# Cross-attention and expert layers on one core: the maxima's mask, the layer norms' root, the counts of a threshold search and a value bias are computed in another way

## The reference, cut to what matters

```python
x = x + attention0(layernorm(x), ctx)             # no mask
x = x + expert_choice(layernorm(x))               # 8 experts, each takes its 1024 best tokens
x = x + attention1(layernorm(x), ctx, mask, pad)  # mask (512 x 64), pad (16 x 64)
x = x + zone_mixture(layernorm(x))                # 8 experts, all tokens

layernorm(x) = (x - mean) / sqrt(var + 1e-5)
# attention1:
V = ctx @ wv.T + bv
attn = softmax(where(pad, where(mask, Q @ K.T / 4, -1e8), -1e8))
out = (attn @ V) @ wo.T + bo
# expert_choice:
Sm = softmax(x @ Wr + br); G, idx = top_k(Sm.T, 1024)
```

## Time and profile before

| | |
|---|---|
| median of three runs | 2231.78 us |
| the profiled execution | 2222.29 us |
| its span in the trace | 2220.6 us |
| TensorE busy | 2063.2 us, 93% |
| VectorE busy | 1386.9 us, 62% |
| ScalarE busy | 937.7 us, 42% |
| GpSimd busy | 357.7 us, 16% |
| attention of layer 0 | 0 to about 378 us |
| search and lists | about 378 to 453 us |
| expert choice's mixture | about 453 to 737 us |
| attention of layer 1 | about 737 to 1140 us |
| zone mixture | from there to the end |

### The profile page before, as it was taken

One profiled execution on the slowest core, in us unless ns is written; L12 is line 12 of the kernel. 1 busy time (PEld: TensorE's weight loads), 2 busy tenths in 40 slices (PEclk: granted clock), 3 DMA queues, 4 the chain that ended last, 5 costly groups with the idle time before them and its releaser, 6 DMA issues.

```text
span 2220.6 us, 38835 instructions
## 1 busy us (share of the span) xinstructions
PE 2063.2 (93%) x14664; PEld 1684.4 (76%) x14665; DVE 1386.9 (62%) x2859; ACT 937.7 (42%) x1405; POOL 357.7 (16%) x351
## 2 busy tenths in 40 slices
PE   7899997589999689999989999999999999999998
PEld 4666665369998456666668888888888888888887
DVE  6888886855555478888768554544545445445444
ACT  3777773055445266666643222222222222222222
POOL 3122211057774311111122000000000000000000
PEclk9999997789999799999989999999999999999999
DMA  3122222045543212222230000000000010010000
GB/s 102 59 85 77 84 68 56 4 128 110 94 78 51 57 39 71 71 72 71 96 133 24 25 29 29 29 29 11 19 29 29 29 29 1 29 29 29 29 10 10
DMA packets 109106, 114.11 MB, mean 51 GB/s; under 512 B 16064, under 2 KB 97728, under 8 KB 108992
## 3 DMA queue, kind: packets, MB, share of 16 engines
q1 hardware_dynamic: 96704, 95.44, 13.5%
q0 software_dynamic: 12288, 17.05, 4.8%
HBM read 61.87 MB, written 50.59 MB: 51 GB/s over the span
## 4 chain that ended last, share of the span: by engine, by line
PE 46%; DVE 2%; ACT 1%; issue 1%; DVEq 0%
PE psum L144 15%; PE psum L145 15%; PE psum L146 15%; DVE zmix_acc L2237 0%; DVE zmix_hid L2246 0%; ACT zmix_hid_hi L2202 0%; ACT L2194 0%; DVE zmix_rest_inh L1882 0%; ACT zmix_act_gate L2194 0%; DVE zmix_rest_zone L1887 0%; DVE zmix_rest_inh L1888 0%; DVE zmix_rest_key L1905 0%; DVE zmix_rest_flag L1907 0%; DVE zmix_rest_key L1904 0%; DVE zmix_rest_best L1906 0%
## 5 line engine op out<-in xcount | busy, mean ns | idle before, releaser
L2246 DVE TENSOR_TENSOR zmix_hid<-zmix_act_gate,psum 128x1024 f32<-128x1024 f32 x128 | 156.3, 1221 | 378.9 <-issue 350.9
L2202 ACT ACTIVATE zmix_hid_hi<-zmix_hid 128x1024 fp32r<-128x1024 f32 x128 | 135.6, 1059 | 394.1 <-PE psum L146 238.8
L2194 ACT ACTIVATE zmix_act_gate<-psum 128x1024 f32<-128x1024 f32 x128 | 131.4, 1027 | 376.3 <-PE psum L146 376.2
L2251 DVE TENSOR_TENSOR zmix_hid_lo<-zmix_hid,zmix_hid_hi 128x1024 fp32r<-128x1024 f32 x128 | 157.7, 1232 | 134.9 <-ACT zmix_hid_hi L2202 133.9
L144 PE MATMUL psum<-zmix_wd_hi,zmix_hid_hi 128*128 128x256 f32 x768 | 217.3, 283 | 2.2 <-DVE zmix_acc L2237 1.9
L145 PE MATMUL psum<-zmix_wd_lo,zmix_hid_hi 128*128 128x256 f32 x768 | 217.2, 283 | 0.0
L146 PE MATMUL psum<-zmix_wd_hi,zmix_hid_lo 128*128 128x256 f32 x768 | 217.1, 283 | 0.0
L2237 DVE SCALAR_TENSOR_TENSOR zmix_acc<-psum,opened_weight,zmix_acc 128x256 f32<-128x256 f32 x512 | 211.6, 475 | 1.6 <-PE psum L146 1.6
L929 ACT ACTIVATE att_probs<-psum 128x512 f32<-128x512 f32 x256 | 135.3, 601 | 92.2 <-PE psum L746 51.6
L1090 DVE TENSOR_REDUCE att_s_max<-psum 128x16 f32<-128x1024 f32 x128 | 152.8, 1216 | 20.6 <-PE psum L712 20.5
L144 PEld LDWEIGHTS psum<-zmix_wd_hi,zmix_hid_hi 128*128 128x128 f32 x768 | 146.8, 191 | 7.4 <-DVE zmix_hid_lo L2251 1.9
(11 more groups left out here) (396 smaller groups left out, 5529.5 us busy)
## 6 DMA issues: line engine op xcount, KB each, us to landing
x<-att_x_new SPq DMA_DIRECT2D x32, 512.0 KB, 2.9
att_x_in<-in_x SPq DMA_DIRECT2D x16, 512.0 KB, 4.0
rows<-att_normed_new SPq DMA_DIRECT2D x16, 512.0 KB, 3.0
att_x_in<-x SPq DMA_DIRECT2D x16, 512.0 KB, 3.9
turned<-att_newT SPq DMA_DIRECT2D x16, 512.0 KB, 2.8
zmix_acc<-x SPq DMA_DIRECT2D x16, 512.0 KB, 4.4
out_x<-zmix_acc SPq DMA_DIRECT2D x16, 512.0 KB, 3.2
moe_wd<-in_w_down SPq DMA_DIRECT2D x8, 768.0 KB, 5.9
```

The lines of the kernel that those rows point to most:

```text
L2194: act.activation(act_gate[:, :, :], psum[:, 0:2, :], ACT.Silu).then_inc(gate_out, 1)
L2202: act.activation(hid_hi[:, e % 2, :, :], hid[:, :, :], ACT.Copy).then_inc(hi_made, 1)
L2246: dve.tensor_tensor(hid[:, :, :], act_gate[:, :, :], psum[:, 2:4, :], ALU.mult).then_inc(up_out, 1)
L2251: dve.tensor_tensor(hid_lo[:, e % 2, :, :], hid[:, :, :], hid_hi[:, e % 2, :, :].bitcast(F32), ALU.subtract).then_inc(lo_made, 1)
```

## The change

Four edits, in both layers' attention, in the search, and in the set-up of layer 1. **Mask:** `masks` uses `mask_cur` as the 64-row stationary matrix and `keysel` as the moving one: 16 products of 64 rows and 128 columns, alternating between the two halves of the array's rows; `mask_tok`, its VectorE instruction, its two inputs and their conversions are gone. **Root:** `layernorm_means` ends with the aggregation; GpSimd (`roots`) adds eps, raises to the power -0.5, and makes the shift, four instructions, between `input_side` and the sum `x_bias`, which becomes `input_bias`; VectorE waits before an aggregation until the last `roots` has read the means. The openings of both layers keep the Newton steps. **Counts:** `count` and `same_e` are fp16. **Value bias:** in layer 1 ScalarE copies the value tiles out of PSUM, without bias; the bias, spread over lanes, is multiplied by `wo` in one product of each half and added to the output bias once.

```diff
+def layernorm_means(dve, xs, parts, stats, mv, sem, start, passed, before, mv_free):
...
+    dve.wait_ge(sem, start + n)
+    mv_free()
+    dve.sem_inc(passed, 1)
+    for k in parts:
+        for t in range(TT):
+            dve.bn_aggr(mv[:, k * TT + t, :], stats[:, k * TT + t, :]).then_inc(sem, 1)
...
-    shared["same_e"] = sc.sb("same_e", [P, E, CHUNKS], side="right")
+    shared["same_e"] = sc.sb("same_e", [P, E, CHUNKS], F16, side="right")
...
-            sp.dma_start(rows32[:, :, :], w["mask_rows"].rearrange("(t p) k -> p t k", p=P)).then_inc(mask_loaded, 16)
-            sp.dma_start(pads32[:, :, :].rearrange("p b k -> p (b k)"), w["pad_rows"].partition_broadcast(P)).then_inc(mask_loaded, 16)
...
-        dve.tensor_scalar(kv["pad_rows"][:, :, :], pads32[:, :, :].bitcast(U8), BIG, -BIG, ALU.mult, ALU.add)
-        dve.tensor_scalar(kv["mask_rows"][:, :, :], rows32[:, :, :].bitcast(U8), BIG, -BIG, ALU.mult, ALU.add)
...
+    def bias_rows(act):
+        for c in range(KC):
+            act.activation(bias_lanes[:, c, :], kv["bv"][:, c:c + 1].to_broadcast([P, P]), ACT.Copy).then_inc(bias_spread, 1)
+
+    def values_copy(act, b):
+        if b == 0:
+            act.wait_ge(v_cleared, 2)
+        act.wait_ge(v_made, b + 1)
+        for a in range(2):
+            rows = slice(a * SK, (a + 1) * SK)
+            heads = psum[rows, v_bank + b % V_BANKS, 0:D].rearrange("p (j a c) -> p j a c", a=2, c=DH)[:, :, a, :]
+            act.activation(kv["v"][rows, b, :, 0:DH], heads, ACT.Copy).then_inc(v_out, 1)
+
+    def value_bias(pe):
+        pe.wait_ge(bias_spread, KC)
+        for c in range(KC):
+            m = pe.matmul(psum[:, 0, 0:D], bias_lanes[:, c, :], wo[:, c, :], start=(c == 0), stop=(c == KC - 1))
+        m.then_inc(bias_made, 1)
+
+    def output_bias(dve):
+        dve.wait_ge(bias_made, 1)
+        dve.tensor_tensor(kv["bo"][:, :], psum[:, 0, 0:D], kv["bo"][:, :], ALU.add).then_inc(bias_out, 1)
...
+            def roots(b):
+                ahead, new = there(b + 2), there(b - 1)
+                pool.wait_ge(ln, ln_start(b) + mean_steps(ahead + new))
...
+                r, s = rstd[:, cols], shift[:, cols]
+                pool.tensor_scalar(r, mv[:, cols, 1], LN_EPS, None, ALU.add).then_inc(rooted, 1)
+                pool.wait_ge(rooted, b * 3 + 1)
+                pool.tensor_tensor(r, r, minus_half[:, cols], ALU.pow).then_inc(rooted, 1)
+                pool.tensor_scalar(s, mv[:, cols, 0], -1.0, None, ALU.mult).then_inc(rooted, 1)
+                pool.wait_ge(rooted, b * 3 + 3)
+                pool.tensor_tensor(s, s, r, ALU.mult).then_inc(shifted, 1)
...
             def body(b, p, half):
                 if there(b + 1):
                     input_side(b + 1, 1 - p, half + p)
+                if there(b + 2) or there(b - 1):
+                    roots(b)
+                if there(b + 1):
+                    input_bias(b + 1, 1 - p, half + p)
...
             def masks(p):
-                for j in range(PAIR_ROWS):
-                    pe.matmul(psum[:, 2 + j, :], const["ident16"][:, :],
-                              mask_tok[:, p, :, :].unsqueeze(2).to_broadcast([P, TT, 2, SK]), start=True, stop=False)
+                for t in range(TT):
+                    for j in range(PAIR_ROWS):
+                        keys = slice(j % 2 * SK, (j % 2 + 1) * SK)
+                        pe.matmul(psum[:, 2 + j, t * P:(t + 1) * P], mask_cur[keys, p, t * P:(t + 1) * P], const["keysel"][keys, :, :],
+                                  start=t == 0, stop=False)
...
-                pads = kv["pad_rows"][:, bass.ds(b, 1), :].to_broadcast([P, TT, SK])
-                dve.tensor_tensor(mask_tok[:, p, :, :], kv["mask_rows"][:, :, :], pads, ALU.min).then_inc(mask_ready, 1)
...
-                layernorm_stats(dve, xs, parts, stats, mv, rstd, tmp, ln, ln_start(b), passed, before)
-                dve.wait_ge(ln, ln_start(b) + steps)
-                cols = slice(0 if ahead else TT, 2 * TT if new else TT)
-                dve.scalar_tensor_tensor(shift[:, cols], mv[:, cols, 0], -1.0, rstd[:, cols], ALU.mult, ALU.mult).then_inc(shifted, 1)
+                layernorm_means(dve, xs, parts, stats, mv, ln, ln_start(b), passed, before, lambda: dve.wait_ge(shifted, b + 1))
...
-        count = sc.sb("count", [P, 1])
+        count = sc.sb("count", [P, 1], F16)
...
             setup["high_parts"](act)
+            setup["bias_rows"](act)
+            for b in range(B):
+                setup["values_copy"](act, b)
...
                     setup["values"](pe, i - 2 * KC)
+                elif i == SETUP_ITEMS:
+                    setup["value_bias"](pe)
...
-                elif 0 <= item < SETUP_ITEMS:
-                    setup["values_out"](dve, item - 2 * KC)
...
-                    setup["pad_masks"](dve)
+                    setup["key_masks"](dve)
                 elif item == SETUP_ITEMS + 3:
-                    setup["key_masks"](dve)
+                    setup["key_pads"](dve)
                 elif item == SETUP_ITEMS + 4:
-                    setup["key_pads"](dve)
+                    setup["output_bias"](dve)
```

More of the change, by code:

```diff
@@ L88, in sem @@
         return self.const["sems"].take(f"{self.phase}_{name}")
+def layernorm_means(dve, xs, parts, stats, mv, sem, start, passed, before, mv_free):
+    n = 0
+    for i, (x, k) in enumerate(zip(xs, parts)):
+        before[i]()
+        for t in range(TT):
+            dve.bn_stats(stats[:, k * TT + t, :], x[:, t, :]).then_inc(sem, 1)
+            n += 1
+    dve.wait_ge(sem, start + n)
[4 more added lines that the diff above has]
+            dve.bn_aggr(mv[:, k * TT + t, :], stats[:, k * TT + t, :]).then_inc(sem, 1)
 def layernorm_stats(dve, xs, parts, stats, mv, rstd, tmp, sem, start, passed, before=()):
@@ L229, in setup_parts @@
     v_made, v_out = sc.sem("v_made"), sc.sem("v_out")
+    bias_spread, bias_made, bias_out = sc.sem("bias_spread"), sc.sem("bias_made"), sc.sem("bias_out")
+    bias_lanes = sc.sb("bias_lanes", [P, KC, P]) if layer == 1 else None
     v_cleared, split_hi, split_lo = sc.sem("v_cleared"), sc.sem("split_hi"), sc.sem("split_lo")
@@ L235, in setup_parts @@
         mask32, pad32 = sc.sb("mask_u8", [P, S // 4], I32), sc.sb("pad_u8", [P, B // 4], I32)
-        rows32, pads32 = sc.sb("rows_u8", [P, TT, SK // 4], I32), sc.sb("pads_u8", [P, B, SK // 4], I32)
-    SMALL = (5 if layer == 0 else 4) * 16
+    SMALL = 5 * 16
     def load(sp, first_rows=None, more_rows=None):
@@ L499, in attention @@
         tmp = sc.sb("ln_tmp", [P, 2, 2 * TT])
+        minus_half = sc.sb("minus_half", [P, 2 * TT])
         mask_cur = sc.sb("mask_cur", [P, 2, S], BF16) if masked else None
[L501 removed]
         x_loaded = [sc.sem(f"x_loaded{p}") for p in range(2)]
@@ L550, in ln_start @@
         def ln_start(b):
-            first = FIRST_LN + ln_steps(1)
+            first = FIRST_LN + mean_steps(1)
             if isinstance(b, int) and b < 1:
@@ L556, in ln_start @@
             if isinstance(b, int) and b > B - 2:
-                return first + (B - 3) * ln_steps(2) + (b - (B - 2)) * ln_steps(1)
-            return b * ln_steps(2) + (first - ln_steps(2))
+                return first + (B - 3) * mean_steps(2) + (b - (B - 2)) * mean_steps(1)
+            return b * mean_steps(2) + (first - mean_steps(2))
         @block.sync
@@ L632, in _ @@
             pool.memset(s_max[:, :, :, :], 0.0).then_inc(cleared, 1)
+            pool.memset(minus_half[:, :], -0.5).then_inc(halves_made, 1)
+            pool.wait_ge(halves_made, 1)
+            def roots(b):
+                ahead, new = there(b + 2), there(b - 1)
+                pool.wait_ge(ln, ln_start(b) + mean_steps(ahead + new))
+                if ahead:
+                    after(pool, norm_in, done(TT, b + 2, 0))
+                if new:
+                    after(pool, norm_out, done(TT, b - 1, 0))
+                pool.sem_inc(passed, 1)
+                cols = slice(0 if ahead else TT, 2 * TT if new else TT)
+                r, s = rstd[:, cols], shift[:, cols]
[5 more added lines that the diff above has]
+                pool.tensor_tensor(s, s, r, ALU.mult).then_inc(shifted, 1)
             def own_values(b, p):
@@ L655, in input_side, with input_bias @@
                     pool.tensor_tensor(out[:, p, :, :, :], cols, own, ALU.mult).then_inc(kb_ready, 1)
+            def input_bias(b, p, half):
+                at_start = isinstance(b, int) and b == 0
                 pool.wait_ge(x_loaded[p], 16 * (half + 1))
@@ L670, in _ @@
                 own_values(0, 0)
-            batches(pool, body)
+            batches(pool, body, roots)
         @block.tensor
@@ L703, in maxima @@
                     if masked:
-                        pe.wait_ge(mask_ready, done(2, b, 2))
+                        pe.wait_ge(mask_ready, b + 1)
                 else:
@@ L1044, in before_input @@
                     dve.wait_ge(x_loaded[p], half * 16 + 32)
-                    after(dve, norm_in, done(TT, b + 2, 0))
```

(2 more changed lines are left out.)

31 lines of the change are left out of this document (16 added, 15 removed).

## The result

The changed kernel takes **2210.98 us** in the median of 6 runs (2202.48 to 2212.55), the kernel before 2229.61 in 6 runs beside it: ratio **0.9906**, 95% interval 0.9882 to 0.9929 (the two medians alone give 0.9916, inside it). A second set of runs gave 0.9903 (0.9888 to 0.9918). The forecast was 2211 us.

A forecast was written before the change was run, and what follows sets the result against it. Layer 0 was taken as a loop including VectorE, layer 1 as a TensorE-ScalarE chain, the search as an engine-to-engine chain. Terms 2.7 + 1.5 + 0.1 + 9.1 + 6.9 = 20.3 us off gave 2211 us on the median's scale, range 2195 to 2228.

The forecast's parts named there:

- Root, layer 0: Layer 0 batches: without Newton steps on VectorE the reciprocal starts 0.19 us earlier; 2.7 us over 14 batches (0 to 4.4).
- Root on GpSimd: GpSimd's four small instructions end 1.1 us after the aggregation, power taken as small (0.2 to 2.38 us); hidden in steady body.
- Ends: Bare chains ending the attentions: Newton and shift's 2.6 us become 1.1 in layer 0, gain 1.5 us; layer 1 gains 0.1.
- Ports: VectorE/GpSimd shared ports: one stall of L114 beside `x_bias` goes; the moved sum beside PSUM readers is charged nothing.
- Mask: `masks` calls on TensorE's chain: 0.67 us instead of 0.96, gain 0.29 a call; 9.1 us in all.
- Counts and values: Search rounds: both edits together cut 0.56 us from read count to decision to 0.30; 6.9 us in all.
- (1): Mask: halves don't hide their weight loads, 1.10 us a call, costing 4.3 us; 2225 us in all, chance 0.17.
- (2): Mask: products neither pair nor hide loads, 1.95 us a call, slower than before at 2251 us; chance 0.07.
- (3): GpSimd root: dear power or blocked queue, 2.2 us lost at layer 0's end and the 2.7 gone; 2216 us, chance 0.13.
- (4): Larger gains: count 0.37 in late and value rounds, layer 0 0.32 a batch, mask 0.4 a call; 2204 us, chance 0.3.

The follow-up runs named there:

- two powers: Changed kernel with a second power, on a scratch tile, ahead of the real one in each GpSimd root step: 2207.46 us, ratio 0.9917 to the kernel before.
- three powers: Changed kernel with two further powers ahead of the real one in each GpSimd root step: 2235.86 us, ratio 1.0047 to the kernel before.
- cheap power: Changed kernel with GpSimd's power replaced by a multiplication of the same operands: 2203.45 us, ratio 0.9908 to the kernel before.
- masks alone: Kernel before with only the new mask, search and roots as before: 2220.87 us, ratio 0.9950 to the kernel before.
- halves apart: Changed kernel with the mask's eight lower-row products first, then the eight upper, not alternating: 2212.95 us, ratio 0.9937 to the kernel before.

## Why the prediction was right, step by step

The sum was right: 20.3 us off was forecast, and measured were 18.6 and 22.1 by the medians of the two sets, 21.0 and 21.6 by their ratios. Its terms were not all right. Layer 0 and its end gave 1.4 us (0.08 in each of 14 batches and 0.33), where I had 4.2. The whole stage can't check this better: the first scan is at 380.2 us in the mean of the five profiles with the Newton steps on VectorE and at 378.9 in that of the five with one power, each group spread over 3 to 5 us, and up to 3.3 of these lie ahead of the first layer norm of the batches (46.6 to 50.0 us), where no edit acts. The search and its exit gave 8.4, where I had 6.9 (search 53.8 us in the three profiles with neither edit, 45.7 in the mean of seven with both; exit 0.4 less). Layer 1 gave 12.2, where I had 9.2 (means of the stage: 404.8 us in the four profiles with the old mask, 392.6 in the seven with the new mask in its own order and at most two powers, whoever makes the roots). A term too large and two too small nearly cancelled, so that the sum came out as well as it did is in part luck.

- **Root, layer 0** (2.7 us, 0 to 4.4). The step "the reciprocal then waits for `turn_values`" held. Its size did not: the reciprocal, and `turn_maxima` with it, moved up by 0.13 us a batch and not by 0.19, and 0.05 of that was lost again behind `turn_maxima`, in every second body. 0.08 us a batch is left, 1.1 us in 14; the period of 19.2 that I named as a sign did not come, it is 19.4. My upper bound was too high as well: two of the 14 listed waits lasted 1.17 us, not one, and the steady ones were 0.22 to 0.28, not 0.32.
- **Root on GpSimd** (1.1 us). This step failed. The power takes 1.67 us for 8 columns and 1.04 for 4, and the hand-over from VectorE 0.22 to 0.37, not 0.16: 3.0 us after the aggregation in the body. I had bounded it by 2.38 and chosen the wrong end: the number of columns was the wrong measure of nearness, the operation was the right one. That cost nothing in the body, since the cover (1.8 us beyond it) was real, as two and three powers show.
- **Ends** (1.5 and 0.1). 0.33 measured at layer 0; with the cheap power 1.19, so the mis-sized power is 0.86 of the difference. The other 0.3 is an instruction that I left out: of GpSimd's four I charged the three that need each other's results, but all four stand in one queue (364.31, 364.68, 364.96 and 365.27 us in the trace of the cheap power). The hand-overs from VectorE and to ScalarE, 0.22 and 0.04 us there, are together what I had charged. The end of layer 1 was not measured by itself.
- **Ports.** One stall went, as said. `x_bias` beside VectorE's reductions of PSUM held none of them: 1.22 to 1.23 us, against 1.21 without it. Charging nothing was right. The largest stall of this kind I had overlooked. In the opening of layer 0, kernel before, and in all five profiles with the Newton steps on VectorE alike:

```profile
47.00 2.35 POOL L662 TENSOR_TENSOR att_x_bias<-att_x_in,att_bo_bcast 128x1024 f32<-128x1024 f32 x1
47.09 2.28 DVE L114 TENSOR_SCALAR att_ln_tmp<-att_mv 128x4 f32<-128x4 f32 x1
```

  The same step takes 0.17 us at the end of the layer; here it ended with GpSimd's sum, 2.1 us later. That stall went with the root, and yet the first period is no shorter (20.04 us before, 20.10 in the changed kernel's first profile), so the period did not hang on it.
- **Mask** (0.29 a call, 9.1 in all). The call start to start shrank by 0.41, yet the period by 0.61 for two calls, 0.31 each: from `turn_values` to the mask it is now 0.10 longer (1.90 against 1.80 us, masks alone against before), the change of the row split that I had charged. So the price of a call was right, and all 32 calls at 0.31 make 9.9. Of the other 2.3 us, 1.2 lie in the opening of the layer, where the clock decides; 1.0 stands behind the last `turn_maxima` of the layer, less than the spread of each group there, and is not explained. The second call of the opening, before and masks alone:

```profile
759.97 1.50 PE L694 MATMUL psum<-att_mask_tok,main_ident 128*128 128x512 bf16 x4 [2.50 <-DVE att_s_max L1090]
```
```profile
772.23 0.62 PE L688 MATMUL psum<-main_keysel,att_mask_cur 64*128 64x128 bf16 x16 [3.27 <-DVE att_s_max L1082]
```

  Start to start these are 1.43 and 0.55 us. The granted clock was 0.65 from 759.9 to 761.5 in the first and 1.00 in the second; a call wholly at 0.50 (1.2 GHz), the opening's first, took 1.71 us before and takes 0.97 in the changed kernel. I had counted 0.4 for one call at half clock and nothing for the other. The second call took 1.19 to 1.51 us in all four profiles with the old mask and 0.55 in all eight with the new one in its own order; why the clock holds there is not shown. From this call to the second `turn_maxima` of the layer it is 2.6 us less (29.9 to 27.3), where three calls at 0.31 make 0.9.
- **Counts and values** (6.9 us). The two-sidedness held to the round (1.69, 1.62, 1.42). The size was 1.5 us short. The late rounds fell by 0.40 where I charged 0.37, the first six by 0.6 to 1.8 in all (13.92 us before; 12.14 and 13.35 in the change's two profiles) where I had 0.5 with rounds 22 and 23, and 0.4 came behind the search, between the last scan and the first expert load, which I had not counted.
- **Rivals.** (1) and (2) are excluded by the 0.027 step and by the halves apart; (3) had the power right and its consequence wrong; (4), larger all round, was nearly as good as the forecast: the search and layer 1 came out on its side in size, layer 0 did not. But its reasons were not the right ones: a value round fell by 0.27 us, as forecast, not by 0.37, and a call by 0.31, not by 0.4.

What hid behind the total is the clock. The first four periods of layer 0 sum to 77.5 to 82.2 us over the profiles (the one with three powers left out): 78.8 to 82.2 with the Newton steps on VectorE, 77.5 to 80.6 without, two groups that overlap. And the changed kernel's first profile has the granted clock at 0.66 from 65 to 70 us where the kernel before has 1.00. An effect under 2 us at an opening is lost in that.

## What to carry over

When two engines finish at the same time, an edit to either one gains almost nothing and the pair gains all; look for the second side before judging the first alone. Before moving work to another engine find the slack in front of its consumer (here 1.8 and 2.95 us): it says what price for an unseen operation still costs nothing. Take the size of a step from the time line and not from a total of waits, which also falls when waits become too short to be listed. And compare stages, not the totals of two profiles, where a stage that nobody touched varies by more than the effect.

## What the runs showed that was not expected

- GpSimd's power of an fp32 tile: 1.67 us for 8 columns and 1.04 for 4, beside 0.20 to 0.21 for a multiplication of the same size, so some 0.16 us for each further column.
- Sixteen products of 64 rows x 128 columns take 0.55 us to the next product when the two row halves alternate and 0.79 when they don't. In both orders the starts form two trains with a step of 0.056 us, weight loads of 0.094 us included; with the halves apart, the second train still begins beside the fifth product of the first.
- A VectorE step on 128 x 4 numbers, 0.17 us at the end of layer 0, lasted 2.28 us beside GpSimd's sum of 128 x 1024 and ended with it.
- The expert stage took from 282.6 to 296.0 us in 13 profiles and differed by 10.7 us between two executions of one kernel.
